# Two attention layers with routed experts on one core: ranks counted in PSUM, causal masks moved between engines, work at the layer ends put in another order

## The reference

```
x = x + attn_a(layernorm(x))      # 16 heads of 8, causal mask, softmax
x = x + ffn(layernorm(x))         # 8 experts 128 -> 512 -> 128, top 2 of 8 per token
x = x + attn_b(layernorm(x))      # 16 heads of 8, no mask, scores scaled by norms of q, k, x
x = x + ffn(layernorm(x))         # the same experts again
```

## Time and profile before

| | us |
|---|---|
| median of 3 runs | 1205.51 (1203.42 to 1205.73) |
| the profiled execution's own time | 1201.22 |
| its span | 1198.8 |
| PE busy | 1031.9 (86%) |
| DVE busy | 763.5 (64%) |
| ACT busy | 672.4 (56%) |
| POOL busy | 538.9 (45%) |

### The profile page before, as it was taken

The page is one execution under the profiler, slowest core; times in us unless marked ns, Lnnn a source line. Parts: engine busy times, 40 slices in busy tenths (PEclk is TensorE's granted clock), DMA queues, the critical chain, the costliest instruction groups (busy, mean ns, idle before and its releaser), DMA issues.

```text
span 1198.8 us, 28758 instructions
## 1 busy us (share of the span) xinstructions
PE 1031.9 (86%) x9198; PEld 719.2 (60%) x9198; DVE 763.5 (64%) x2364; ACT 672.4 (56%) x1399; POOL 538.9 (45%) x1010
## 2 busy tenths in 40 slices
PE   3998999896789989999798879998977689899990
PEld 1444555452358889999444434443443489899990
DVE  5687777968548333366778888888767573234442
ACT  2465767553524445555377769887836445455550
POOL 2243444333850630344688645655626416103555
PEclk9999999996858999999778889998967799999995
DMA  6355444662125877887644324333121258778974
GB/s 158 92 133 142 100 103 98 179 140 61 40 70 154 267 230 235 258 270 221 143 110 100 97 56 108 82 92 84 44 56 58 91 171 282 217 227 263 280 218 111
DMA packets 201722, 175.02 MB, mean 146 GB/s; under 512 B 19812, under 2 KB 160616, under 8 KB 201576
## 3 DMA queue, kind: packets, MB, share of 16 engines
q1 hardware_dynamic: 193384, 156.41, 47.4%
q0 software_dynamic: 8192, 16.79, 4.7%
HBM read 122.99 MB, written 50.14 MB: 144 GB/s over the span
## 4 chain that ended last, share of the span: by engine, by line
PE 44%; DVE 15%; POOL 9%; issue 6%; DMA 4%; SPq 1%; ACT 1%; POOLq 0%; ACTq 0%; DVEq 0%
PE psS L1358 9%; PE psT L1365 9%; PE psO L316 4%; PE psN L1381 4%; PE psO L1381 4%; PE psS L350 3%; POOL xn L1259 3%; DVE mx L662 3%; POOL prow L736 2%; PE psO L959 2%; PE psN L323 1%; PE psT L358 1%; PE psM L1346 1%; DMA eo<-ysb 1%; POOL part L749 1%
## 5 line engine op out<-in xcount | busy, mean ns | idle before, releaser
L662 DVE TENSOR_REDUCE mx<-psS 128x3 f32<-128x384 f32 (+1 forms) x512 | 311.1, 617 | 117.9 <-PE psS L377 62.4
L350 PE MATMUL psS<-kst,qst 48*128 48x256 bf16 (+1 forms) x1024 | 200.9, 284 | 57.2 <-DVE mx L662 42.6
L549 ACT ACTIVATE pT<-psT,scb 128x512 f32<-128x512 f32 x256 | 194.0, 778 | 56.7 <-PE psT L358 55.3
L1421 DVE TENSOR_TENSOR hT<-sg,psT 128x512 f32<-128x512 f32 x142 | 97.5, 686 | 160.3 <-PE psT L1365 126.1
L358 PE MATMUL psT<-qst,kst 50*128 50x256 bf16 (+1 forms) x1024 | 194.0, 279 | 5.4 <-DMA qst<-scr_m 2.4
L1245 POOL DMA_INDIRECT xg<-xn,slot x128 | 123.5, 965 | 149.9 <-DVE ysb L1416 86.5
L780 POOL TENSOR_SCALAR_AFFINE_SELECT pT<-pT 128x256 f32<-128x256 f32 x256 | 104.0, 414 | 134.0 <-ACT pT L544 132.2
L350 PEld LDWEIGHTS psS<-kst,qst 48*128 48x128 bf16 x1024 | 65.7, 97 | 156.8 <-DVE mx L662 82.7
L1358 PE MATMUL psS<-xTt,wgc 128*128 128x128 f32 x1136 | 153.5, 279 | 5.0 <-issue 5.0
L544 ACT ACTIVATE pT<-psT 128x384 f32<-128x384 f32 x256 | 122.6, 491 | 57.7 <-PE psT L358 56.2
L1365 PE MATMUL psT<-xTt,wuc 128*128 128x128 f32 x1136 | 151.8, 277 | 0.4 <-DMA wuc<-in_L_ffn_Wu 0.3
(11 more groups left out here) (227 smaller groups left out, 1605.2 us busy)
## 6 DMA issues: line engine op xcount, KB each, us to landing
wgc<-in_L_ffn_Wg SPq DMA_DIRECT2D x142, 256.0 KB
wuc<-in_L_ffn_Wu SPq DMA_DIRECT2D x142, 256.0 KB
scr_part<-part SPq DMA_DIRECT2D x128, 128.0 KB, 2.1
qst<-scr_part SPq DMA_DIRECT2D x64, 192.0 KB, 3.7
kst<-scr_part SPq DMA_DIRECT2D x64, 192.0 KB, 4.5
xin<-xg SPq DMA_DIRECT2D x142, 64.0 KB
eo<-ysb SPq DMA_DIRECT2D x142, 64.0 KB
scr_part<-part SPq DMA_DIRECT2D x32, 192.0 KB, 1.9
```

What stands on the lines that cost most here:

```text
L350: return nc.tensor.matmul(ps[:, c0:c0 + n], q_[r64, t, q0], k_[r64, t, 0:n], start=(half == 0), stop=True, skip_group_check=True)
L549: nc.scalar.activation(pT[:, g % 8, 0:cols], psT[g % 2][:, 0:cols], ACT.Exp, scale=scb[r][:, 0, i:i + 1], bias=scb[r][:, 1, i:i + 1]).then ...
L662: nc.vector.tensor_reduce(mx3[:, u, 0:n, pos:pos + 1].rearrange("p a b -> p (a b)"), psS[h % 2][:, 0:kcols(L)].rearrange("p (a k) -> p a k ...
L1421: nc.vector.tensor_tensor(out=hT[(n0 + k) % FETCH][:].rearrange("p a c -> p (a c)"), in0=sg[p][:], in1=psT[p][:], op=ALU.mult).then_inc(f[ ...
```

## The change

- `pe_counts`: after the `triu` matmul, 16 matmuls with ones add the picks of block k to the columns of all later blocks, in PSUM (start=False). The result is the rank itself, with two more groups of 8 columns: the total, and the total of the first 8 blocks. `dve_counts` copies 144 columns instead of 256. Stage 3 and the first two operations of stage 6 are gone. `further` goes to `lg`.
- Group 1: stages 4 to 8 move up in `dve_route`, and `pool_ffn` waits for one tile less for every scatter.
- The exponentials of the last two batches of layer A are masked by a matmul of an identity with `tritb` into psT (MASKED = 14); `pv_quad` waits for the exponentials, and POOL has no selects there. The second transposed score matmul of a causal head no longer has start=True. POOL builds `tritb` at the start, and PE and DVE wait for it.
- Group 0: stages 4 to 7 follow the counts at once. Stage 8 and then stage 2 move to the end of step 18, in both layers.
- The layer norm of 12 blocks in step 18 is spread over heads 0 to 8, its tokens over heads 10 to 13.
- Layer B: POOL's 16 token blocks (in step 15, ahead of `pool_split`) become 8 at the end of step 14 and 8 at the end of step 15, behind `pool_split`.
- ACT loads the silu table in the tile loop, after the first two token copies.

```diff
@@ pv_quad
-                after(pe, s["pT"], 16 * b + 4 * q + 4)
+                if L.causal and b >= MASKED:
+                    after(pe, s["exp"], 16 * b + 4 * q + 4)
+                else:
+                    after(pe, s["pT"], 16 * b + 4 * q + 4)
@@ pe_step
                     last_t = scores_t(1)
+                    if L.causal and bT >= MASKED:
+                        diag = psT[1 - par][:, 0:3 * P].rearrange("p (a k) -> p a k", a=3)[:, 0:3:2, :]
+                        last_t = nc.tensor.matmul(diag, identb[:], tritb[:].unsqueeze(1).to_broadcast([P, 2, P]),
+                                                  start=False, stop=True, skip_group_check=True)
@@ pool_step
-                    nc.gpsimd.affine_select(out=d, in_=d, compare_op=ALU.is_ge, fill=0.0, base=0,
-                                            pattern=[[0, 2], [1, P]], channel_multiplier=-1).then_inc(s["pT"], 1)
+                    if bT < MASKED:
...
@@ pe_counts
-            nc.tensor.matmul(count_bank(n)[:, w:2 * w], onesb[:], rhs, start=True, stop=True,
-                             skip_group_check=True).then_inc(r["cnt_ps"], 1)
+            for k in range(size):
+                upper = size + 2 if k < PART else size + 1
+                last = nc.tensor.matmul(bank[:, k + 1:upper, :], onesb[:],
+                                        pickb[:, k:k + 1, :].to_broadcast([P, upper - k - 1, E]),
+                                        start=False, stop=True, skip_group_check=True)
+            last.then_inc(r["cnt_ps"], 1)
@@ dve_route
             if k == ROUTE_CNT:
                 dve_counts(dve, n)
-                dve_route_part(dve, n, 3)
+                dve_route_part(dve, n, 4)
             if k == ROUTE_BASE:
-                dve_route_part(dve, n, 4)
                 dve_route_part(dve, n, 5)
+                dve_route_part(dve, n, 6)
             if k == ROUTE_SLOT:
-                dve_route_part(dve, n, 6)
+                dve_route_part(dve, n, 7)
             if k == ROUTE_SLOT + 1:
-                dve_route_part(dve, n, 7)
-            if k == ROUTE_SLOT + 2:
                 dve_route_part(dve, n, 8)
@@ pool_ffn
-                    pool.wait_ge(f_sem["y"], n0 + ROUTE_SLOT + pair // 2)
+                    pool.wait_ge(f_sem["y"], n0 + ROUTE_SLOT - 1 + pair // 2)
                 else:
-                    pool.wait_ge(f_sem["u"], n0 + ROUTE_SLOT + 3 + pair // 2)
+                    pool.wait_ge(f_sem["u"], n0 + ROUTE_SLOT + 2 + pair // 2)
@@ pool_beside
-                if l == 1 and j == 15 and h == 1:
+                if l == 1 and j in (14, 15) and h == H:
                     pool.wait_ge(s_ln[2], 1)
-                    for k in range(SIZE[0]):
+                    for k in range((j - 14) * SIZE[0] // 2, (j - 13) * SIZE[0] // 2):
@@ dve_beside
-                if l == 0 and j == 16 and h < 6:
-                    dve_route_part(dve, 0, h + 3)
+                if l == 0 and j == 16 and h < 4:
+                    dve_route_part(dve, 0, h + 4)
...
-                if j == 18 and h in (6, 8):
-                    if h == 6:
+                if j == 18 and h == 15:
+                    dve_route_part(dve, n, 8)
+                    dve_route_part(dve, n, 2)
+                if j == 18:
+                    if h == 0:
                         dve.wait_ge(x1, NBLK - 4)
-                        dve_ln_stats(dve, SIZE[0], NBLK - 4, s_ln[n + 1])
-                        dve.wait_ge(s_ln[n + 1], 1)
-                    else:
-                        dve_tokens(dve, n + 1, SIZE[0], NBLK - 4)
+                    dve_ln_at(dve, h, SIZE[0], NBLK - 4 - SIZE[0], s_ln[n + 1], 1)
+                    if 10 <= h < 14:
+                        dve_tokens(dve, n + 1, SIZE[0] + 3 * (h - 10), SIZE[0] + 3 * (h - 9))
```

More of the change, by code:

```diff
@@ L40 @@
 PCH = 23
+MASKED = B - 2
 POS = [8 * (h // 8) + 4 * (h % 2) + (h % 8) // 2 for h in range(H)]
@@ L146, in build @@
         pickb = sb("pickb", [P, SIZE[0], E], BF16)
-        counts = sb("counts", [P, 2, SIZE[0], E])
+        counts = sb("counts", [P, max(SIZE) + 2, E])
         v12 = sb("v12", [P, 3, SIZE[0]])
@@ L358, in scores_t @@
                     return nc.tensor.matmul(ps[:, c0:c0 + T - q0], k_[m64, t, half * P:half * P + P], q_[m64, t, q0:T],
-                                            start=True, stop=True, skip_group_check=True)
+                                            start=(half == 0 or not L.causal), stop=True, skip_group_check=True)
                 if S_:
@@ L1024, in dve_counts @@
             size = SIZE[n % G]
-            nc.vector.tensor_copy(counts[:, :, 0:size, :],
-                                  count_bank(n)[:, 0:2 * size * E].rearrange("p (a k e) -> p a k e", a=2, e=E)).then_inc(r["cnt"], 1)
+            nc.vector.tensor_copy(counts[:, 0:size + 2, :].rearrange("p k e -> p (k e)"),
+                                  count_bank(n)[:, 0:(size + 2) * E]).then_inc(r["cnt"], 1)
             dve.wait_ge(r["cnt"], n + 1)
@@ L1119, in dve_route_part @@
                 link(nc.vector.tensor_tensor(out=w[:, 1, :], in0=w[:, 0, :], in1=e_, op=ALU.mult))
[L1120 to L1133 removed]
+            rank, total, part = counts[:, 0:size, :], counts[:, size, :], counts[:, size + 1, :]
+            a, b, further = ea_, eb_, lg[:, 0:size, :]
             down, up = upto[:, 0, 0, :], upto[:, 0, 1, :]
@@ L1396, in act_tile @@
                 tokens(1)
+                nc.scalar.activation(junk[0:1, 0, 0:1], ones_row[0:1, 0:1], ACT.Silu)
             if live(k, 0):
@@ L1626, in hook @@
                     act_tokens(act, 2 * l + 1, h // 2)
-                if j == 19 and h == 15:
-                    nc.scalar.activation(junk[0:1, 0, 0:1], ones_row[0:1, 0:1], ACT.Silu)
                 if l == 0 and j == 19 and h == 14:
@@ L1760, in _ @@
                                     pattern=[[-1, P]], channel_multiplier=1).then_inc(s_const, 1)
+            nc.gpsimd.affine_select(out=tritb[:], in_=tritb[:], compare_op=ALU.is_ge, fill=NEG, base=0,
+                                    pattern=[[1, P]], channel_multiplier=-1).then_inc(s_const, 1)
             for r in range(RING):
```

47 lines of the change are left out of this document (17 added, 30 removed).

## The result

The changed kernel takes **1164.85 us** (median of 4 runs, 1163.32 to 1166.68) against 1205.62 us before (4 runs, 1203.42 to 1211.88): a ratio of 0.9654, 95% interval 0.9614 to 0.9694, so 3.5% faster. The forecast was 1176, its range 1165 to 1191: the direction was right, the gain too small, and the time lies 0.15 us under the range. The profiled execution took 1166.68 us, 34.5 us less than that of before (1201.22); the sum of the prediction was 28.1.

A forecast was written before the change was run, and what follows sets the result against it. PE bounds mid-pipeline steps; in the last steps it waits for DVE, POOL and the layer norm, at lower clock. A 12.4, B 9.1 and ffn 6.6 sum to 28.1 us, giving 1173.1 or 1177.4; forecast 1176, range 1165 to 1191.

The forecast's parts named there:

- Step 16 of A: Layer A: DVE loses 6.2 us of routing work, PE's counts cost 1.5; gain 4.0 us (2 to 5).
- Step 17 of A: Layer A: 2.8 us of waits for POOL's selects go, masks cost 2.4, clock returns 0.6; gain 1.0 (-2 to 2.8).
- so up to 1.4; I take 0.6: Step 17 of layer A: fewer stops let PE's clock hold better, worth up to 1.4 us, taken as 0.6.
- 0.30 is the upper price, 0 the lower; I take half: Step 17 of layer A: each of 16 mask matmuls costs PE 0.15 us, 2.4 us a step.
- Step 18 of A: Layer A: waits for POOL's selects and the residual behind the layer norm go; 21.3 to 16.3 us, gain 5.0 (1 to 8).
- Step 19 and the first tile of A: End of layer A: fewer POOL waits and better clock, 2.0 us (-1 to 4); later silu table load, 0.4.
- Layer B: Steps 15 to 18: token blocks 2.5, shorter DVE route 2.1, step 18 4.1, silu table load 0.4; gain 9.1 us.
- The named cover: End of layer B: 32 scatters take 39.3 us; slots come 2.5 + 3.0 us earlier, scatters allow about 9.5, just enough.
- The ffn: Both layers: last scatter a tile sooner, 5.6 us (3.5 to 6); first tiles 1.0 (-1 to 2); 6.6 together.
- the clock holds: Rival: steps 16 to 19 at full clock in both layers, some 10 us more gained, 1166 us; chance 0.11.
- PE is the next bound, at the low clock: Rival: remaining stops keep PE's clock at 0.6, masks and counts cost more, gain 16 us, 1189 us; chance 0.23.
- slower: Rival: ACT and PE issue refill the waits, masks and counts stand bare, only ffn's 5.6 won; 1219 us, chance 0.04.

The follow-up runs named there:

- short stand-ins: Group 0's scatters replaced by POOL operations of 0.69 us: kernel before 1197.88 us; changed kernel 1163.19 us, or 1169.79 us with POOL masking batches 14 and 15.
- long stand-ins: Changed kernel, group 0's scatters replaced by POOL operations of 1.06 us: 1163.27 us; with POOL masking batches 14 and 15 as well, 1177.34 us.

## Why the prediction was right or wrong

**Step 16 of A, 4.0 forecast, 5.5 measured.** Right in kind, but the counts were priced too high. The rows of their weight loads (minimum, median, maximum in ns):

```profile
L983 PEld LDWEIGHTS psM<-pickb,onesb x32: 98/137/152, 277.2 to 866.4; 128*128 128x128 bf16 x32
...
L983 PEld LDWEIGHTS psO<-pickb,onesb x32: 95/98/99, 354.3 to 934.2; 128*128 128x128 bf16 x32
```

The time isn't the sum of these rows, since the loads overlap. PE's rows of the 16 matmuls and of the next head, with the change, and of the one matmul before it:

```profile
277.26 1.19 PE L983 MATMUL psM<-pickb,onesb 128*128 128x136 bf16 x16
278.38 0.28 PE L355 MATMUL psS<-kst,qst 48*128 48x128 bf16 x1
```

```profile
274.09 0.31 PE L969 MATMUL psM<-pickb,onesb 128*128 128x128 bf16 x1
...
274.33 0.28 PE L350 MATMUL psS<-kst,qst 48*128 48x128 bf16 x1
```

The next head comes 1.12 us after the first of the 16, at clock 0.50, and came 0.24 us after the one of before: 0.9 us for the counts, where the sum took 1.5 and called 0.5 possible if loads overlap better. In the ffn, at clock 1.00, the 16 take 0.6 us. The sign "the 16 count matmuls within 1.5 to 2.4 us" failed on the good side. These 0.9 us fall ahead of step 16, in the 1.9 by which step 15 got longer; the forecast had booked them in step 16, so 4.6 stand against its 4.0. The Trainium skill, "TensorE: Matmul & The Clock Gate", section LDWEIGHTS, gives such a load as its column count over 1.2 GHz, 107 ns, and doesn't mention the clock. The 98 ns of the second row come near it, the 137 of the first don't; and 16 loads in a row, which would be 1.7 us by it, took 1.1 and 0.6. The measurement decides.

**Step 17 of A, 1.0 forecast, 4.4 measured.** This is the step of the prediction that failed, in two terms. The larger is "so up to 1.4; I take 0.6" for the clock. It set PE's 16.95 us against the 15.56 of a step in mid pipeline, which holds more work. The kernel before with short stand-ins does the work of this very step in 14.05 us at clock 1.00, so the term is 2.9. The other is "0.30 is the upper price, 0 the lower; I take half" for a mask: 0.075 to 0.08 is what the runs with all masks on PE and with short stand-ins show, so 1.3 in place of 2.4 us. With these two 2.8 + 2.9 - 1.3 = 4.4. The range given (-2 to 2.8) was too narrow by its own terms too: 2.8 of wait, 1.4 of clock and masks for nothing would be 4.2.

**Step 18 of A, 5.0 forecast, 7.7 measured**, by the same two sizes: PE's work took 13.3 us where the forecast had 14.9 + 2.4 - 1.5 = 15.8. That the norm's cover had to go too was right: with the norm in one piece and short stand-ins a wait of 6.3 us stands in its place.

**Step 19 and the first tile of A, 2.4 with the silu table, 4.7 measured.** The long stand-ins show that this whole difference can come from the stops of step 18. The forecast read the like stretch of B for it and took a third of its 4.8 us.

**Layer B, 9.1 forecast, 12.3 measured, after 2.1 lost ahead of step 16.** The token blocks are worth 5.1, by one run on a chip that isn't quiet, where 2.5 were forecast. Step 18 gained 6.2 where 4.1 were forecast, at clock 1.00. The named cover did end: POOL's 32 scatters run nearly back to back,

```profile
878.19 1.11 POOL L1245 DMA_INDIRECT xg<-xn,slot  x1 [22.76 <-ACT pT L558]
...
918.42 0.96 POOL L1245 DMA_INDIRECT xg<-xn,slot  x1 [0.30 <-issue]
```

and PE waits for the first tokens:

```profile
922.65 0.45 PE L1346 MATMUL psM<-ident,xin 128*128 128x128 f32 x1 [3.06 <-DMA xin<-xg]
```

"Just enough" was short by this wait. The runs with stand-ins take 15.7 to 16.7 us for this stretch against 18.2, so 1.5 to 2.5 us; the two traces of the kernel before, 16.4 and 20.1, lie further apart than that, so whether the stretch lost anything to the kernel before isn't shown. POOL's 40 us are the next bound of that layer's end.

**The ffn, 6.6 forecast, 0.0 and 3.5 measured.** The scatter's wait is worth a tile, as putting it back shows, but the two layers kept different parts of it. In the first ffn the last scatter, then SP's next token load:

```profile
412.63 0.96 POOL L1245 DMA_INDIRECT xg<-xn,slot  x1 [0.30 <-issue]
```

```profile
416.94 0.33 SPq L1442 DMA_DIRECT2D xin<-xg  x1
```

4.3 us lie between them, where it was 2.4 before (433.29 to 435.71). So the earlier scatter took 1.9 us longer until SP went on, and here it falls on the weight loads of 411.94 to 412.8; that those delay it wasn't tried. PE's wait for the tokens shrank from 1.75 to 0.6 us. The 1.0 us of the first tiles wasn't there: ten tiles take 32.1 us, as before. But the first ffn of the kernel before is itself 2.7 us longer in its second trace, so the 0.0 can't be told from the forecast by this pair.

**The signs.** No wait of PE for POOL is left in layer A beyond step 16, DVE no longer waits for POOL's chain in step 16 of B, and the wait for tokens at tile 25 is under 1 us: these held. Of the signs of being wrong one came, PE waiting for the first tile's tokens in layer B.

**The rivals.** The number of the one called "the clock holds", 1166 us, is what was measured, chance given 0.11; its condition, steps 16 to 19 at full clock in both layers, isn't. Steps 17 and 18 of A and 18 of B ran at 1.00, the five other stretches at 0.64 to 0.82. The chips that are not quiet show 0.980, which would be 1182 here: between the forecast (0.976) and "PE is the next bound, at the low clock" (0.986, given 0.23), but with the waits without a sender, which neither has. The mistake was to price the clock step by step as a share of a gain: in the rows of 2 us it is 1.00 or 0.50, and between only where it changes, and steps 17 and 18 kept the upper level throughout. But stops alone don't tell when it falls. In the ffn of before it stays at 1.00 around the wait of 1.75 us, and in step 15 of A, with the change, it falls although PE is busy all the time, when the small matmuls of the logits come:

```profile
262.00:264.00 2.00, 2.00 (x22) 1.82 (x21) 0.74 (x2) 0.49 (x1) 0.41 (x1) 1.00 1.21 159
264.00:266.00 2.00, 2.00 (x20) 1.13 (x23) 0.69 (x2) 0.95 (x3) 0.41 (x1) 0.75 0.19 27
266.00:268.00 2.00, 2.00 (x22) 0.62 (x14) 0.82 (x3) 0.73 (x3) 0.41 (x1) 0.50 0.00 0
```

It does the same in step 16 of B at 858 to 862 us, which the rival named as what speaks against it. The rival "slower" had nothing for it: PE's idle time was waits. On which side of the range's end the time fell, by 0.15 us, is chance, since the four runs lie 3.4 us apart; and that the sum was off by only 5.8 of the 33.9 us between the traces is luck in part. The steps that it treats at the two layers' ends gained 15.2 us more than it had, while the ffns gained 3.1 less and 6.2 were lost ahead of step 16 in both layers, of which it had only the counts, and those in another place. Of the 11.2 us between 1176 and 1164.85, 6.4 are the sum's error between the two traces; of the rest, 2.9 are what the forecast added because the median of before lay over its profiled execution, and 1.8 that with the changed kernel it lay under it.

## What to carry to other kernels

Where the engine that sets the pace lowers its clock around stops, waits can be worth more than their own length: here 4.2 us of net waits gave 12.1, of which 4.8 in the stretch behind. So forecast such an edit as two cases, the clock kept or lost, and don't average them; and take the work at full clock from a trace of the same step, not of another. The price of a small added matmul is read from a stretch in which its engine is full (0.075 us), not from its row (0.28 us), and that of a chain from the start of its first to the start of what follows (1.1 us for 16 whose loads last 2.2 together). What an edit at the end of a queue is worth is bounded by the next queue in line (POOL's 40 us of scatters).

## What the runs showed of the hardware that I had not expected

The same program takes 1165 us on one chip and 1229 on another, and the kernel before 1205 to 1210 on three and 1252 on three, while single instructions last nearly as long on both kinds (the scores' matmuls 0.286 and 0.289 us in the mean, the indirect DMAs 0.962 and 0.960). The others have waits of up to 5.4 us in which ACT, DVE and POOL get no release that the trace shows; 125 to 160 us of engines' idle time in each of the twelve traces, all in stretches with indirect DMAs, none in the eight traces from quiet chips. Whether the DMAs cause them stays open: the kernels with stand-ins that were to tell it all ran on quiet chips. The worth of the parts may shift with the kind of chip as well: on these the masks by PE show no gain, while undoing the ranks costs 7 to 14 us against other edits on the same chips.

In a chain of 16 matmuls with the same 128-column weights the starts lie 58 to 25 ns apart at clock 1.00 (first ffn) and 114 to 27 at 0.50 (layer A), closer as the matmuls move fewer columns (136 down to 8), though each load's row lasts 95 to 98 and 104 to 152 ns.
